# Layer 0's feed-forward reordered: pairs of tiles, all first rotations first, relu on VectorE, one clamp less

## What is computed

```python
def act_quant(x, bits):
    qb = 2.0 ** (bits - 1) - 1.0
    scale = qb / jnp.clip(jnp.max(jnp.abs(x), axis=-1, keepdims=True), 1e-05, None)
    q = jnp.clip(jnp.round(x * scale), -qb, qb) / scale
    ...
def hbitlinear(x, w, bits):
    xh = fwht(x)                      # Walsh-Hadamard transform of the last dimension
    xq = act_quant(xh, bits)
    wq = weight_quant(w)              # ternary
    return jnp.einsum('bsh,oh->bso', xq, wq)
...
h = hbitlinear(hidden_states, w_up, 8)      # 256 -> 512
h = jnp.square(jax.nn.relu(h))
out = hbitlinear(h, w_down, 8)              # 512 -> 256
...
x = _layernorm(x + out, axis=-1)
```

## Time and profile before

| | |
|---|---|
| median of 3 runs | 911.53 us (910.24 to 914.83) |
| the profiled execution's own time | 913.34 us |
| its span, first to last instruction | 911.6 us |
| mean granted clock of TensorE | 0.91 |
| busy over the span | PE 777.1, DVE 618.8, ACT 468.4, POOL 458.9 us |

### The profile page before, as it was taken

The page is one execution under the profiler, slowest core; times in us unless marked ns, Lnnn a source line. Parts: engine busy times, 40 slices in busy tenths (PEclk is TensorE's granted clock), DMA queues, the critical chain, the costliest instruction groups (busy, mean ns, idle before and its releaser), DMA issues. The chain is left out here.

```text
span 911.6 us, 18363 instructions
## 1 busy us (share of the span) xinstructions
PE 777.1 (85%) x5783; PEld 485.0 (53%) x5786; DVE 618.8 (68%) x2095; ACT 468.4 (51%) x1480; POOL 458.9 (50%) x459
## 2 busy tenths in 40 slices
PE   6799889885765999999999999997574499999954
PEld 4566666664542444555555555786454354554423
DVE  2646677794584777788888888332245768878766
ACT  2466776571662000588888888100232176766634
POOL 4344564462360666566666665000630468878840
PEclk9859999997895999999999999999785589999986
DMA  9400000000000567500000000241449222222216
GB/s 326 166 1 1 2 2 1 1 2 0 1 1 13 141 154 188 165 1 1 1 2 1 2 1 1 104 173 42 140 167 225 99 62 71 74 70 65 74 38 202
DMA packets 32495, 63.45 MB, mean 70 GB/s; under 512 B 6592, under 2 KB 21324, under 8 KB 31536
## 3 DMA queue, kind: packets, MB, share of 16 engines
q1 hardware_dynamic: 20960, 41.67, 14.2%
q0 software_dynamic: 4896, 11.95, 4.2%
q10 hardware_dynamic: 6544, 8.67, 3.6%
HBM read 41.27 MB, written 9.84 MB: 56 GB/s over the span
## 5 line engine op out<-in xcount | busy, mean ns | idle before, releaser
L1353 ACT ACTIVATE a_room<-a_room,a_nm 128x257 f32<-128x257 f32 x256 | 127.3, 500 | 100.5 <-DVE a_nm L1203 99.7
L1391 POOL TENSOR_TENSOR a_room<-a_room,a_rd 128x1024 f32<-128x1024 f32 x64 | 121.3, 1895 | 65.8 <-DVE a_rd L1211 65.4
L1203 DVE CUSTOM_DVE_ANT_0 a_room<-a_ps,table,NSK 128x256 f32<-128x256 f32 x256 | 107.9, 479 | 0.4 <-PE a_ps L1062 0.4
L613 POOL TENSOR_TENSOR l_Pr<-l_Pr,l_rd 128x256 f32<-128x256 f32 (+1 forms) x80 | 82.0, 1043 | 51.9 <-DVE l_rd L501 51.8
L584 ACT ACTIVATE l_Pr<-l_Sm,l_nm 128x128 f32<-128x128 f32 (+1 forms) x192 | 88.4, 462 | 37.7 <-DVE l_nm L487 23.6
L1062 PE MATMUL a_ps<-room 64*128 64x256 f32 x512 | 72.3, 402 | 0.5 <-DVE a_nm L1203 0.5
L1142 PE MATMUL a_ps<-a_room,W 128*128 128x512 f32 x160 | 71.9, 607 | 0.8 <-ACT a_room L1367 0.8
L1062 PEld LDWEIGHTS a_ps<-room 64*128 64x128 f32 x512 | 44.1, 186 | 53.2 <-issue 48.5
L1183 DVE SCALAR_TENSOR_TENSOR a_room<-a_ps,BQK,table 128x512 f32<-128x512 f32 x80 | 56.4, 747 | 22.2 <-PE a_ps L1142 21.6
L1077 PE MATMUL a_ps<-table,a_room 128*128 128x128 f32 x512 | 69.7, 279 | 1.1 <-ACT a_room L1362 1.1
L1090 PE MATMUL a_psO<-a_room,room 128*64 128x512 f32 x256 | 68.8, 617 | 0.0
(11 more groups left out here) (311 smaller groups left out, 1836.8 us busy)
## 6 DMA issues: line engine op xcount, KB each, us to landing
room<-a_room SPq DMA_DIRECT2D x96, 64.0 KB, 2.1
room<-a_room ACTq DMA_DIRECT2D x96, 64.0 KB, 2.1
room<-in_w_in SPq DMA_DIRECT2D x1, 6144.0 KB, 18.2
room<-in_c_in SPq DMA_DIRECT2D x1, 4096.0 KB, 12.4
room<-pairs SPq DMA_DIRECT2D x8, 512.0 KB, 7.5
W<-in_w SPq DMA_DIRECT2D x1, 3072.0 KB, 12.5
room<-in_w_out SPq DMA_DIRECT2D x1, 3072.0 KB, 19.6
W<-in_wo SPq DMA_DIRECT2D x1, 2048.0 KB, 9.3
```

The costliest lines, as they stand in the source:

```text
L613: last = pool.tensor_tensor(p, p, r.unsqueeze(2).to_broadcast([P, n, n_keys]), ALU.mult)
L1203: nc.vector.tensor_tensor_reduce(out=Sm[:, t % 2, n, 0:S], in0=psS(t)[:, n // 2, n % 2, :], in1=c["window"][:, n % 2, :], scale=-1.0, scal ...
L1353: nc.scalar.activation(Pr[:, t % 4, n, :], Sm[:, t % 2, n, :], ACT.Exp, bias=nm[:, t % 2, n:n + 1], scale=-1.0, accum_out=den[:, t % 2, n: ...
L1391: pool.tensor_tensor(p, p, rd[:, t % 2, :].unsqueeze(2).to_broadcast([P, 4, S]), ALU.mult).then_inc(normed, 1)
```

## The change

The computation of the block stays the same, except that the clamps to +-127 in front of the rounding are gone. `MAGIC` is added in the multiplying instruction, so a tile's values take one DVE instruction instead of two.

- **Pairs.** `x_turn`, `keep_xt`, `rotate`, `quantise1`, `round1`, `q_turn` and `keep_q1` work on two tiles in each instruction or group. POOL's mixing and `quantise2` work on the pairs (0,1), (2,3), (4,5) and then on tiles 6 and 7 alone.
- **Order.** The lists are written out by hand. PE does all four pairs of `x_turn` and `rotate` first, into four banks of `psR`; then for all eight tiles `up`, `h_turn` and `rotate2`; and then for all eight `q2_turn` and `down`. `psX` and `psH` become two banks `psXH`; `psQ2` and `psY` reuse two of `psR`'s banks.
- **Relu** moves from ACT to DVE (`max` with 0, without the scale). The square is of unscaled integers; `quantise2` multiplies its maximum and its scale by `unit`, which is `dq` squared times the norm factor.
- **Norm.** `apply` is split: tiles 0 to 5 after `take(6)`, tiles 6 and 7 after `take(7)`. A square root of one element at the head of ACT's list brings its table in early.

```diff
...
+        PAIRS, MIXES = NT // 2, ((0, 1), (2, 3), (4, 5), (6,), (7,))
...
+        psXH = st.ps("ff_psXH", [P, 2, 512])
+        psR = st.ps("ff_psR", [P, 4, 512])
         psU = st.ps("ff_psU", [P, 512])
+        psQ2 = psR[:, 2, :].bitcast(BF16)
+        psY = psR[:, 3, 0:D]
...
+            def x_turn(p):
+                need(pe, s["xt"], p - 1)
+                for i in range(2):
+                    for k in range(KD):
+                        last = nc.tensor.transpose(psXH[:, p % 2, (2 * i + k) * P:(2 * i + k + 1) * P],
+                                                   X[:, 2 * p + i, k * P:(k + 1) * P], ident[:, :])
...
+            def rotate(p):
+                pe.wait_ge(s["xt"], p + 1)
+                if p == 0:
+                    pe.wait_ge(loads["had"], 16)
+                for i in range(2):
+                    for k in range(KD):
+                        last = nc.tensor.matmul(psR[:, p, i * D:(i + 1) * D], xt[:, p, i, k, :], HAD[:, k, 0:D],
+                                                start=(k == 0), stop=(k == KD - 1))
...
-            in_slots([(rotate, 1), (x_turn, 0), (rotate2, 5), (h_turn, 4), (up, 3), (q_turn, 2), (down, 8),
-                      (q2_turn, 7)])
+            x_turn(0)
+            x_turn(1)
+            rotate(0)
+            x_turn(2)
+            rotate(1)
+            x_turn(3)
+            rotate(2)
+            rotate(3)
+            for n in range(NT + 2):
+                if n < NT:
+                    if n % 2 == 0:
+                        q_turn(n // 2)
+                    up(n)
+                if 0 <= n - 1 < NT:
+                    h_turn(n - 1)
+                if 0 <= n - 2:
+                    rotate2(n - 2)
+            q2_turn(0)
+            for t in range(NT):
+                if t + 1 < NT:
+                    q2_turn(t + 1)
+                down(t)
...
-            def relu(t):
-                act.wait_ge(s["up"], t + 1)
-                nc.scalar.activation(hr[:, :], psU[:, :], ACT.Relu,
-                                     scale=dq[:, 0, t:t + 1]).then_inc(s["hr"], 1)
+            def square(t):
                 act.wait_ge(s["hr"], t + 1)
-                need(act, s["hT"], t)
-                nc.scalar.activation(h[:, :], hr[:, :], ACT.Square).then_inc(s["h"], 1)
+                need(act, s["hT"], t - 1)
+                nc.scalar.activation(h[:, t % 2, :], hr[:, t % 2, :], ACT.Square).then_inc(s["h"], 1)
...
-            in_slots([(keep_xt, 0), (keep_rot2, 5), (keep_h, 4), (relu, 3), (keep_q1, 2), (keep_q2, 7),
-                      (round1, 1), (round2, 6)])
-            ln.root(act)
+            def root(n, tiles):
+                act.wait_ge(ln.has_var, n + 1)
+                nc.scalar.activation(ln.std[:, tiles], ln.mv[:, tiles, 1], ACT.Sqrt,
+                                     bias=c["eps"][:, 0:1]).then_inc(ln.has_std, 1)
+
+            nc.scalar.activation(warm[:, 0:1], c["ones"][:, 0:1], ACT.Sqrt)
+            for p in range(PAIRS):
+                keep_xt(p)
+            round1(0)
+            keep_q1(0)
+            square(0)
+            round1(1)
+            square(1)
+            keep_h(0)
+            keep_q1(1)
+            for n in range(1, NT):
+                if n + 1 < NT:
+                    if n in (1, 3):
+                        round1((n + 3) // 2)
+                    if n in (3, 5):
+                        keep_q1((n + 1) // 2)
+                    square(n + 1)
+                keep_h(n)
+                keep_rot2(n - 1)
+            keep_rot2(NT - 1)
+            round2(0)
+            round2(1)
+            for t in range(NT):
+                keep_q2(t)
+                if t + 2 < NT:
+                    round2(t + 2)
+                if t == 6:
+                    root(0, slice(0, 6))
+            root(1, slice(6, 8))
...
+            for tiles in MIXES:
+                on, n = slice(tiles[0], tiles[-1] + 1), len(tiles)
+                pool.wait_ge(s["rot2c"], tiles[-1] + 1)
+                pool.tensor_tensor(half[:, 0:n, 0::2, :], z[:, on, 0::2, :], z[:, on, 1::2, :], ALU.add)
+                link(pool.tensor_tensor(half[:, 0:n, 1::2, :], z[:, on, 0::2, :], z[:, on, 1::2, :], ALU.subtract))
+                pool.tensor_tensor(full[:, on, 0:2, :], half[:, 0:n, 0:2, :], half[:, 0:n, 2:4, :], ALU.add)
+                link(pool.tensor_tensor(full[:, on, 2:4, :], half[:, 0:n, 0:2, :], half[:, 0:n, 2:4, :],
+                                        ALU.subtract))
+                pool.sem_inc(s["mixed"], 1)
...
-                    out, src, sc[:, i, t:t + 1], 127.0, ALU.mult, ALU.min)))
-                each(lambda i, t, src, out, norm, done: nc.vector.tensor_scalar(
-                    out, out, -127.0, MAGIC, ALU.max, ALU.add).then_inc(s[done], 1))
...
+            def quantise1(p):
+                on = slice(2 * p, 2 * p + 2)
+                dve.wait_ge(s["rot"], p + 1)
+                link(nc.vector.tensor_reduce(am[:, 0, on], psR[:, p, :].rearrange("p (i d) -> p i d", i=2), AX.X,
+                                             ALU.max, apply_absolute_value=True))
+                link(nc.vector.tensor_scalar(m[:, 0, on], am[:, 0, on], rd0, 1e-5, ALU.mult, ALU.max))
+                link(nc.vector.reciprocal(rc[:, 0, on], m[:, 0, on]))
+                link(nc.vector.tensor_scalar(sc[:, 0, on], rc[:, 0, on], 127.0, rd0, ALU.mult, ALU.mult))
+                for i in range(2):
+                    last = nc.vector.tensor_scalar(q1[:, p, i, :], psR[:, p, i * D:(i + 1) * D],
+                                                   sc[:, 0, 2 * p + i:2 * p + i + 1], MAGIC, ALU.mult, ALU.add)
+                last.then_inc(s["q1"], 1)
+                link(nc.vector.tensor_scalar(dq[:, 0, on], m[:, 0, on], wsc[:, 0:1], 1.0 / 127.0, ALU.mult, ALU.mult))
+                link(nc.vector.scalar_tensor_tensor(out=unit[:, on], in0=dq[:, 0, on], scalar=rd1, in1=dq[:, 0, on],
+                                                    op0=ALU.mult, op1=ALU.mult))
+
+            def relu(t):
+                dve.wait_ge(s["up"], t + 1)
+                need(dve, s["h"], t - 1)
+                nc.vector.tensor_scalar(hr[:, t % 2, :], psU[:, :], 0.0, None, ALU.max).then_inc(s["hr"], 1)
+
+            def quantise2(n):
+                tiles = MIXES[n]
+                on = slice(tiles[0], tiles[-1] + 1)
+                dve.wait_ge(s["mixed"], n + 1)
+                link(nc.vector.tensor_reduce(am[:, 1, on], full[:, on].rearrange("p i k t -> p i (k t)"), AX.X,
+                                             ALU.max, apply_absolute_value=True))
+                link(nc.vector.tensor_tensor(m[:, 1, on], am[:, 1, on], unit[:, on], ALU.mult))
+                link(nc.vector.tensor_scalar(m[:, 1, on], m[:, 1, on], 1e-5, None, ALU.max))
+                link(nc.vector.reciprocal(rc[:, 1, on], m[:, 1, on]))
+                link(nc.vector.scalar_tensor_tensor(out=sc[:, 1, on], in0=rc[:, 1, on], scalar=127.0, in1=unit[:, on],
+                                                    op0=ALU.mult, op1=ALU.mult))
+                for t in tiles:
+                    nc.vector.tensor_scalar(q2[:, t, :], full[:, t].rearrange("p k t -> p (k t)"),
+                                            sc[:, 1, t:t + 1], MAGIC, ALU.mult, ALU.add).then_inc(s["q2"], 1)
+                link(nc.vector.tensor_scalar(dq[:, 1, on], m[:, 1, on], wsc[:, 1:2], 1.0 / 127.0, ALU.mult, ALU.mult))
...
+                ln.stat(t, last=t in (5, 7))
+
+            def apply(n, tiles):
+                dve.wait_ge(ln.has_std, n + 1)
+                link(nc.vector.reciprocal(ln.rstd[:, tiles], ln.std[:, tiles]))
+                for t in range(tiles.start, tiles.stop):
+                    nc.vector.tensor_scalar(X[:, t, :], ln.R[:, t, :], ln.mv[:, t, 0:1], ln.rstd[:, t:t + 1],
+                                            ALU.subtract, ALU.mult).then_inc(ln.normed, 1)
+
+            quantise1(0)
+            quantise1(1)
+            relu(0)
+            relu(1)
+            quantise1(2)
+            relu(2)
+            relu(3)
+            quantise1(3)
+            relu(4)
+            relu(5)
+            quantise2(0)
+            relu(6)
+            relu(7)
+            quantise2(1)
+            take(0)
+            take(1)
+            quantise2(2)
+            take(2)
+            take(3)
+            quantise2(3)
+            take(4)
+            take(5)
+            quantise2(4)
+            take(6)
+            apply(0, slice(0, 6))
+            take(7)
+            apply(1, slice(6, 8))
```

178 lines of the change are left out of this document (58 added, 120 removed).

## The result

| | median of 20 runs | from | to | profiled execution, its span |
|---|---|---|---|---|
| before | 911.13 us | 907.91 | 915.00 | 913.34, 911.6 |
| after | 914.70 us | 908.82 | 923.79 | 919.79, 917.9 |

A forecast was written before the change was run, and what follows sets the result against it. No engine was full over the whole block; DVE bounded its steady part. The steps summed to 65.1 us against 67.0; with 0.8 off the gain and an allowance for the profiled execution, 911.2 us, 8-in-10 range 906.5 to 916.5.

The forecast's parts named there:

- Fill, to 228.0: Block's start: all first rotations up front, PE dense from 218.2, clock rising near 222, last rotation ending at 228.0.
- First half, to 243.6: From 228.0 through up, relu, square, turn and rotation to the end of POOL's mixing of the first pair, 5.2 us.
- To 247.5: quantise2 of the pair ... 3.2 in sum: After the first mixing: DVE's second quantising of the first pair, 3.2 us, then the relu of tile 6, 0.7.
- To 252.8 and 257.8: Seven ACT instructions, tile 7's second rotation and copy to 252.8; then round2, transposes, down and two takes to 257.8.
- Three links, 18.5 us: Second half, to 276.3: each take waits through PE's list for a later tile's quantising; 6.0 us a link, first 6.5.
- The pair's link: The first of the second half's three serial links, with a pair of tiles instead of one, put at 6.5 us.
- End, 4.9 us: Block's end: six apply, take(7), the root and two reciprocals, two apply; 4.9 us, to 281.2.
- It pays only where DVE was the bound: Removing the clamps takes 5.3 and about 2.8 us from DVE, but gains time only where DVE bounds the block.
- The fall of the clock: Rival: PE's clock drops at about 235 and stays down, 918 to 920 us; with late rise instead, 916; chance 0.13.
- Rival 3: POOL's mixing is the bound: over 20% longer instructions delay the second half's links by 1 to 2 us; 913, chance 0.10.
- The relu's move: First half: eight relus of 0.69 us, 5.5 us in all, taken from ACT and given to DVE.

The follow-up runs named there:

- a_down_first: The kernel after with PE doing down(t) ahead of q2_turn(t+1), and ACT's list reordered to match; ratio to before 0.9986.
- b_no_clamps: The kernel before with only the clamps removed, MAGIC added in the multiplying instruction; 903.31 us, ratio to before 0.9936.
- a_clamps_back: The kernel after with the clamps of both quantisings put back; ratio to before 1.0112.
- a_one_column: The kernel after with DVE's small operations on a pair's two numbers, except the reciprocal, done one column at a time; ratio to before 0.9995.
- a_pe_busy: The kernel after with extra unused matmuls that fill PE's waits; ratio to before 1.0020.
- a_no_mix: The kernel after with POOL's mixing left out, quantise2 reading the copied rotation directly; ratio to before 0.9958.
- a_pool_in_fill: The kernel after with 14 unused POOL additions beside the first quantisings; one execution without a ratio, one 128x2 multiplication took 1.14 us instead of 0.17.
- a_mix_by_tile: The kernel after with POOL mixing tile by tile in shorter instructions instead of pairs; ratio to before 1.0041.
- a_relu_first: The kernel after with the relus of tiles 6 and 7 ahead of quantise2(0) in DVE's list; ratio to before 1.0017.

## Why the prediction was wrong, step by step

- **Fill, to 228.0.** Right. The last rotation of after ends at 227.95, and the clock rose near 222 as assumed.
- **First half, to 243.6.** Right within 0.2 us. The relu on DVE takes 0.69, POOL's pair instructions 1.26 to 1.28, and `quantise2(0)` starts at 243.39.
- **"To 247.5: quantise2 of the pair ... 3.2 in sum".** This step failed. It measured 6.9. The reduction was right (1.22). The four small ones were priced from the row of reciprocals of one number per partition (0.160) and took 0.16, 1.13, 0.17 and 0.99. The two multiplications were put at 0.5 each and took 2.97 together. The row behind the 0.5 said 0.594 on average with POOL beside it, and the prediction took the low end. The spread was there to be read in the trace of before, where the same instruction took 0.49 us alone and 0.98 beside POOL.

Timeline of before:

```profile
247.34 0.49 DVE L858 TENSOR_SCALAR ff_q<-ff_full,ff_sc 128x512 f32<-128x512 f32 x1
...
254.01 0.73 POOL L829 TENSOR_TENSOR ff_full<-ff_half 128x256 f32<-128x256 f32 x1
254.04 0.98 DVE L858 TENSOR_SCALAR ff_q<-ff_full,ff_sc 128x512 f32<-128x512 f32 x1
```

- **To 252.8 and 257.8.** `quantise2(2)` starts at 263.25 instead of 257.8. Of these 5.4 us, 3.6 are the step above (250.36 for `relu(6)` instead of 246.8). The other 1.9 go by behind it, at first with the clock at 0.50 (`up` 1.01 instead of 0.60).
- **Three links, 18.5 us.** Right: from 263.25 to 282.64, where `apply` starts behind `take(6)`, it is 19.4. a_down_first shows that the order of the lists costs 4.5 us here. The pair's link beside POOL held some of the same waits (0.65 for L910, 0.56 for L912), which the forecast had left out.
- **End, 4.9 us.** Right: 282.64 to 287.23, 4.6 us.
- **"It pays only where DVE was the bound".** Right for the old order, wrong for the new. In the old order the removal gained 5.8 us, and the steady part went from 3.79 us for a tile to between 3.2 and 3.5 (b_no_clamps). In the new order, where DVE isn't full in the second half (3.75 of 5 us in 265 to 270), it is still worth 7.0 us (a_clamps_back): there DVE's quantising lies on the path. The sum had stepped the new order without clamps and so wasn't touched by this. But the sentence hid that the change holds one gain of 6 to 7 us and other parts that lose 9.
- **Rivals.** The fall of the clock came, near 250 and not at 235, behind PE's wait for DVE: in a_one_column, without most of that wait, the clock is 1.00 in 250 to 255. What it is worth stays open (a_pe_busy, 1.4 us, not clear of nothing). Rival 3 had the right pair of engines and the wrong mechanism: POOL wasn't late, but its running instructions held DVE up. The relu's move was priced as work shifted from ACT to DVE; in the old order it alone costs 5.8 us, most likely by what then stands ahead of it. What it costs in the new order no run shows.

Shown by runs are the wait for POOL as a mechanism (a_no_mix, a_pool_in_fill), its price in the small operations with what follows from it (a_one_column, 3.6 us, as much as the whole loss against before), and the price of the second half's order (4.5). Open are the share of the two wide multiplications, which no run separated, the share of the clock, and why a_mix_by_tile gained nothing.

## What to carry to other kernels

A mean duration from a row with another engine beside it is a mix of two lengths. Before that row prices a step, look at its single instances, and at which of them the new order will produce. When an engine is to do more of its work while another runs beside it, price its instructions by their longest instance, and keep small per-partition numbers in instructions of one column where they can be. A change with several parts is best tried part by part: here the plain removal alone gained 0.6%, and one more bank in the old order 0.8% on top, while the new order around it lost 1%.

## What the runs showed of the hardware

- While POOL runs an instruction between SBUF operands, a DVE multiplication that starts later and reads and writes SBUF with two or more numbers per partition waits until that instruction ends. In after, instructions on 128x2 of 0.16 to 0.22 us took up to 1.18 (L895) and 1.24 (L917), and ended 0.01 to 0.03 us behind POOL's. One that started 0.01 us ahead of POOL's took its own 0.16 (L898 of a_pool_in_fill). Multiplications with one number per partition (0.34 for two, inside POOL's instruction), reciprocals (0.17), reductions (1.21 in a_relu_first), and instructions that read PSUM (0.88 for two, 0.69) didn't wait. The Trainium skill, page "SBUF — State Buffer", section "Who interferes with whom", gives the rule: the two engines share one pair of ports, and whichever comes first holds it for its whole instruction, if DVE's instruction is in a two-port mode or has two inputs in SBUF (the latter against an instruction of POOL that reads SBUF, as all of these do). By that rule reductions stay out of it; the trace agrees. It doesn't name reciprocals, which stayed out too.
- That it begins with as little as two columns was the surprise. The Trainium skill, page "VectorE: DVE Perf Modes", section "Mode 2×_2P — use both read ports for one tensor", asks for operands in SBUF, which keeps readers of PSUM out, and for an outermost dimension longer than one that is even (or odd and equal for source and destination). Two columns meet that, and the 1.13 us of L910 agree. The page doesn't say what holds for a single column; that it stays out is what the L924 of a_one_column shows (0.34 for two).
- POOL is held up in turn: its L873 took 1.44 us in after beside DVE's wide multiplication and 1.28 where DVE read PSUM.
